# Moving work within a batch on all five engines: an attention stage with a hand-written order, Trainium2, one core

## The reference

```python
x = x + jnp.tanh(g_xattn[0]) * _L0_xattn_ref(_layernorm(x), ctx_1024, ctx_1024, w_q, b_q, w_k, b_k, w_v, b_v, w_o, b_o)
x = x + jnp.tanh(g_ffn[0]) * _L0_ffn_ref(_layernorm(x), conf_w, conf_b, gate_w, up_w, down_w, wealth)

# attention: softmax(q k^T / sqrt(16)) v per head, then w_o
# ffn:
bids = sigmoid(x @ conf_w.T + conf_b) * wealth          # (b, s, 8)
top_bids, selected = top_k(bids, 2)
combine = sum(one_hot(selected, 8) * softmax(top_bids)[..., None], axis=2)
expert_out[e] = (silu(x @ gate_w[e].T) * (x @ up_w[e].T)) @ down_w[e].T
output = einsum('ebsh,bse->bsh', expert_out, combine)
```

## Time and profile before

| | us |
|---|---|
| median of 3 runs | 1151.61 |
| lowest and highest | 1150.68, 1152.59 |
| profiled execution | 1148.98 |
| its span, first to last instruction | 1147.2 |
| prologue, to the end of the first turned maxima | 0 to 44.4 |
| batches 0 to 2 | 44.4 to 124.6 |
| one batch of the steady loop | 24.9 |
| batch 14 | 398.3 to 424 |

### The profile page before, as it was taken

The page is one execution under the profiler, slowest core; times in us unless marked ns, Lnnn a source line. Parts: engine busy times, 40 slices in busy tenths (PEclk is TensorE's granted clock), DMA queues, the critical chain, the costliest instruction groups (busy, mean ns, idle before and its releaser), DMA issues. The chain is left out here.

```text
span 1147.2 us, 24335 instructions
## 1 busy us (share of the span) xinstructions
PE 1069.5 (93%) x8310; PEld 892.5 (78%) x8310; DVE 647.4 (56%) x1575; ACT 547.4 (48%) x877; POOL 347.4 (30%) x404
## 2 busy tenths in 40 slices
PE   5789999999999978898999999999899999999994
PEld 4556767777777755575999999999579999999993
DVE  3657777777777764447444444444754444444442
ACT  4466777777777744445333333333643333333331
POOL 2024545554545552513112112112311211211211
PEclk8799999999999989999999999999999999999997
DMA  7000111111111173466212112112461211211211
GB/s 240 25 21 20 50 39 43 63 38 38 47 38 38 49 272 146 141 240 225 58 23 38 33 23 38 33 23 38 160 234 19 38 33 23 38 33 23 38 33 16
DMA packets 48426, 79.41 MB, mean 69 GB/s; under 512 B 6400, under 2 KB 42240, under 8 KB 44544
## 3 DMA queue, kind: packets, MB, share of 16 engines
q0 software_dynamic: 18080, 50.93, 16.5%
q1 hardware_dynamic: 30304, 27.95, 8.3%
HBM read 53.42 MB, written 25.18 MB: 69 GB/s over the span
## 5 line engine op out<-in xcount | busy, mean ns | idle before, releaser
L1809 POOL DMA_INDIRECT out<-y,token x64 | 103.7, 1620 | 473.3 <-DVE y L1693 352.7
L1585 ACT ACTIVATE silu<-gate 128x512 f32<-128x512 f32 x128 | 76.8, 600 | 277.0 <-PE up L1424 277.0
L960 DVE TENSOR_REDUCE max_neg<-maxps 128x4 f32<-128x1024 f32 x128 | 156.5, 1223 | 56.1 <-PE maxps L547 56.0
L1436 PE MATMUL down<-w_split,h_hi 128*128 128x512 f32 x512 | 185.8, 398 | 0.0
L1684 DVE TENSOR_TENSOR h<-silu,up 128x512 f32<-128x512 f32 x128 | 88.1, 688 | 171.0 <-ACT silu L1585 171.0
L1424 PE MATMUL gate<-x_hi,w_split 128*128 128x256 f32 x1024 | 184.1, 281 | 0.0
L1424 PE MATMUL up<-x_hi,w_split 128*128 128x256 f32 x1024 | 184.0, 281 | 0.0
L759 ACT ACTIVATE probs<-scores 128x1024 f32<-128x1024 f32 x124 | 127.3, 1026 | 86.4 <-PE scores L572 85.2
L1424 PEld LDWEIGHTS gate<-x_hi,w_split 128*128 128x128 f32 x1024 | 148.8, 188 | 2.9
L1424 PEld LDWEIGHTS up<-x_hi,w_split 128*128 128x128 f32 x1024 | 147.8, 188 | 0.0
L1438 PE MATMUL down<-w_split,h_lo 128*128 128x256 f32 x512 | 144.0, 281 | 0.0
(11 more groups left out here) (203 smaller groups left out, 1762.5 us busy)
## 6 DMA issues: line engine op xcount, KB each, us to landing
xg<-dispatched SPq DMA_DIRECT2D x39, 272.0 KB, 2.8
stage<-gate_T POOLq DMA_DIRECT2D x10, 1024.0 KB, 7.2
stage<-up_T POOLq DMA_DIRECT2D x10, 1024.0 KB, 9.4
stage<-down_T POOLq DMA_DIRECT2D x10, 1024.0 KB, 11.5
ctxT<-ctxT SPq DMA_DIRECT2D x17, 256.0 KB, 2.9
x_all<-x SPq DMA_DIRECT2D x16, 256.0 KB, 5.1
out<-x_all SPq DMA_DIRECT2D x16, 256.0 KB, 2.1
out<-y,token POOLq DMA_INDIRECT x70, 3.8
```

Of the source, the lines that this page charges most:

```text
L960: V.tensor_reduce(to, maxps[:], AX.X, ALU.max, negate=True).then_inc(s["max_taken"], 1)
L1436: mm(down[t][:].rearrange("p (n d) -> p n d", n=2), h_hi[:, i, rows], split[:, :, cols], start=i == 0, stop=False, skip_group_check=True)
L1585: nc.scalar.activation(silu[pair % 2][:], gate[pair % 2][:], ACT.Silu).then_inc(s_silu, 1)
L1809: pool.indirect_dma_start(out, bass.IndirectOffsetOnAxis(token[:, t:t + 1], axis=0), y[:, t, :], None, compute_op=ALU.add).then_inc(s_adde ...
```

## The change

The orders of the five engines' slots change; no operation is added or dropped but the places of waits.

- TensorE: `max_scores` 3 goes ahead of `score` 3, `score` 5 and `max_scores` 4 go behind the ranks, and the stack K0 behind the second group of values (`weigh` 1). `UNITS` follows: S5 now ahead of K0.
- ScalarE: the dense keys are read ahead of the third exponential instead of behind the fourth, the first values' result ahead of the fourth instead of behind the fifth, the sixth exponential ahead of K0's reading.
- VectorE: the statistics of x ahead of the first choice, and the positions ahead of the maxima of pair 5 instead of behind them.
- GpSimd: bias and contexts' split in mid-batch, ahead of the split of Q and the scatters, instead of behind both. In batch 1 the contexts' split for batch 3 goes directly behind the split of K.
- Prologue: stacks in the order K0, Q0, K1, Q1, the first maxima of batch 0 as soon as the first three are there, batch 1's norm, transpose and projections between them.

```diff
-        UNITS = ["S0", "S1", "S2", "S3", "S4", "K0", "S5", "S6", "S7", "K1", "Q0", "Q1"]
-        STACKS = ["K0", "K1", "Q0", "Q1"]
+        UNITS = ["S0", "S1", "S2", "S3", "S4", "S5", "K0", "S6", "S7", "K1", "Q0", "Q1"]
+        STACKS = ["K0", "Q0", "K1", "Q1"]
...
-            for what in STACKS:
-                stack_first(0, what)
+            stack_first(0, "K0")
+            stack_first(0, "Q0")
+            stack_first(0, "K1")
+            max_scores(0, 0, 0, 2)
+            turn_x(1, PRO1)
+            stack_first(0, "Q1")
+            max_scores(0, 0, 1, 2)
+            project_k(1, 1, PRO1)
+            max_scores(0, 0, 2, 2)
             pe.wait_ge(s["consts_loaded"], 16 * NCONST)
             pe.wait_ge(s["constants_ready"], 1)
-
             project_v(0, PRO1)
-            turn_x(1, PRO1)
-            max_scores(0, 0, 0, len(STACKS))
-            project_k(1, 1, PRO1)
-            max_scores(0, 0, 1, len(STACKS))
+            max_scores(0, 0, 3, 2)
             project_q(PRO1)
...
                 weigh(b, par, 0)
+                max_of_next(3)
                 score(b, par, 3)
-                max_of_next(3)
                 if back:
                     attn_out(use)
                 score(b, par, 4)
-                max_of_next(4)
...
                 if late:
                     ranks(b - 2, use)
+                score(b, par, 5)
+                max_of_next(4)
+                weigh(b, par, 1)
                 stack_ahead("K0")
-                weigh(b, par, 1)
                 max_of_next(5)
-                score(b, par, 5)
...
                 exps(b, 0)
                 exps(b, 1)
+                if ahead:
+                    read_k(b + 2, use)
                 exps(b, 2)
...
+                read_pv(b, 0)
                 exps(b, 3)
                 if ahead:
-                    read_k(b + 2, use)
                     norm_x(b + 2)
...
                 max_of_next(4)
-                max_of_next(5)
                 if late:
                     positions(b - 2, par, use)
+                max_of_next(5)
...
+                if isinstance(b, int) and b == 1:
+                    split_ctx(3, 1, use)
                 if back:
                     scale_of(b - 1, "scale2_chain", "ln2_stats", mv2, rstd2, shift2, "ln2_scaled")
+                if ahead:
+                    add_bias(b + 2)
+                if ahead and not is_first(b):
+                    split_ctx(b + 3, 1 - par, use)
                 if ahead:
                     split(b + 2, "Q", use, units_before(b) + (UNITS.index("Q1") + 1 - len(UNITS)))
                 if late:
                     scatter(b - 2, par)
-                if isinstance(b, int) and b == 1:
-                    split_ctx(3, 1, use)
-                if ahead and not is_first(b):
-                    split_ctx(b + 3, 1 - par, use)
-                if ahead:
-                    add_bias(b + 2)
```

More of the change, by code:

```diff
@@ L311, in attention_stage @@
         PRO0 = Use(["TX", "K", "Q"], 0)
-        PRO1 = Use(["V", "TX", "K", "Q", "MT"], after_all(PRO0))
+        PRO1 = Use(["TX", "K", "V", "Q", "MT"], after_all(PRO0))
         def without(*parts):
@@ L651, in tensor_attention @@
             project_v(0, PRO1)
-            turn_x(1, PRO1)
-            max_scores(0, 0, 0, len(STACKS))
-            project_k(1, 1, PRO1)
-            max_scores(0, 0, 1, len(STACKS))
+            max_scores(0, 0, 3, 2)
             project_q(PRO1)
-            for pair in range(2, HPAIRS):
+            pe.wait_ge(s["unit_read"], len(STACKS))
+            max_scores(0, 0, 4, len(STACKS))
+            for pair in range(5, HPAIRS):
+                stack_first(1, STACKS[pair - 5])
                 max_scores(0, 0, pair, len(STACKS))
-                if pair < 6:
-                    stack_first(1, STACKS[pair - 2])
             turn_maxima(0, PRO1)
+            stack_first(1, STACKS[3])
             def body(b, par, use, ahead, nxt, back, late):
@@ L829, in scalar_attention, with read_first_stack @@
             act.wait_ge(s["consts_made"], 1)
[L830 to L841, removed]
+            def read_first_stack(b, what):
+                read_stack(b, what[0], int(what[1]), first_stack_unit(b, what))
+            norm_x(0)
+            read_whole(xT[:], "TX", PRO0)
+            read_k(0, PRO0)
+            high_part(0, "K", PRO0)
+            read_q(0, PRO0)
+            high_part(0, "Q", PRO0)
+            read_first_stack(0, "K0")
+            norm_x(1)
+            read_first_stack(0, "Q0")
+            read_first_stack(0, "K1")
+            read_whole(xT[:], "TX", PRO1)
+            read_first_stack(0, "Q1")
+            read_k(1, PRO1)
+            high_part(1, "K", PRO1)
+            act.wait_ge(s["consts_loaded"], 16 * NCONST)
+            nc.scalar.activation(tg[:], gates[:], ACT.Tanh).then_inc(s["consts_made"], 1)
+            read_q(1, PRO1)
+            high_part(1, "Q", PRO1)
+            for what in STACKS:
+                read_first_stack(1, what)
             def body(b, par, use, ahead, nxt, back, late):
@@ L852, in body @@
                     read_whole(oT[:], "TN", use)
+                read_pv(b, 0)
                 exps(b, 3)
                 if ahead:
-                    read_k(b + 2, use)
                     norm_x(b + 2)
                 exps(b, 4)
+                exps(b, 5)
                 if late:
                     second_weight(b - 2)
-                read_pv(b, 0)
                 if ahead:
@@ L863, in body @@
                 stack_ahead("K0")
-                exps(b, 5)
                 if back:
@@ L875, in body @@
                 stack_ahead("K1")
+                stack_ahead("Q0")
                 if back:
                     sigmoid(use)
-                stack_ahead("Q0")
+                read_pv(b, 3)
                 stack_ahead("Q1")
-                read_pv(b, 3)
             def out_of_last():
@@ L1062, in vector_attention @@
             dve.wait_ge(s["constants_ready"], 1)
+            for pair in range(3):
+                maxima(0, pair)
+            rest_part(1, "K")
             dve.wait_ge(s["consts_loaded"], 16 * NCONST)
@@ L1066, in vector_attention @@
             read_v(0, PRO1)
-            for pair in range(HPAIRS):
+            maxima(0, 3)
+            maxima(0, 4)
+            rest_part(1, "Q")
+            for pair in range(5, HPAIRS):
                 maxima(0, pair)
[L1069 to L1074, removed]
+                if pair < 7:
+                    split_weights(pair - 5, "kv"[pair - 5], (wk_s, wv_s)[pair - 5])
             read_maxima(0, PRO1)
@@ L1083, in body @@
                     space_early_experts(use)
+                if ahead:
+                    stats_x(b + 2)
                 if late:
                     first_choice(b - 2)
-                if ahead:
-                    stats_x(b + 2)
                 if nxt:
```

## The result

The changed kernel is slower: 1207.29 us (median, 1206.47 to 1208.67) against 1151.14 for the kernel before; the ratio is 1.0488, 95% interval 1.0459 to 1.0517. The profiled execution took 1206.47 (span 1204.8) against 1148.98: +57.5, where the forecast had +35.8. The direction and the place were right; the time lies 7 us above the range.

A forecast was written before the change was run, and what follows sets the result against it. TensorE, busy 93% of the span, was taken as the bound. Prologue -5.0, batches 0, 1 and 14 -0.8, batch 2 -4.0 and loop +45.6 sum to +35.8: 1184.8 profiled, forecast 1187.4 us, range 1171 to 1200.

The forecast's parts named there:

- The hold: Loop batches: large GpSimd operations hold VectorE's two-SBUF-input operations in positions, delaying max_scores 6; 2.4 us a batch, order gain included.
- The small operations: GpSimd's four 128x2 operations beside positions' first operations hold nothing; charged nothing, against 0.5 us a batch by the skill.
- second_choice: VectorE, loop: the earlier K_rest holds its two-input operations, ending it about 1.0 us later; TensorE feels 0.15.
- The clock: TensorE, loop: matmuls run at 1.2 GHz behind an idle stretch of about 2.7 us; 1.4 us a batch, bounds 0 and 2.2.
- batch 2's 1.4 us: The part of batch 2's extra 3.96 us in the old trace put on the slow clock behind its 2.24 us gap.
- The order by itself: Loop batches: the new order without the GpSimd hold gains about 0.24 us a batch, bounds -0.4 and +0.1.
- K_rest's gap: TensorE's 0.35 us wait for GpSimd's K_rest ahead of the keys' first stack, forecast to go.
- the new wait of 0.3 for the fourth exponential: TensorE, loop: score 5, now close behind score 4, must wait about 0.3 us for the exponential of 4.
- Batch 2's stall: Batch 2: first_choice no longer meets the contexts' splits on GpSimd; -4.0 us, bounds -4.4 and 0.
- The prologue: Before the loop: first maxima behind three stacks bring turn_maxima from 43.44 to 38.3; -5.0 us, bounds -8 and -2.5.
- The first rival: Loop: VectorE is held but the slow clock costs nothing; 12 x 2.4 less 9.8 = +19.0, 1170.6 us; chance 0.22.
- the train: GpSimd's bias, context's high part and rest, run in sequence at 217.05 to 220.4 beside VectorE's positions in a loop batch.

The follow-up runs named there:

- e7: The changed kernel with GpSimd's contexts' split directly behind the scale of x and the bias directly behind the split of K: 1140.43 us, ratio 0.9919.
- e11: e10 with GpSimd's loop order of e7, so the old loop order on TensorE, ScalarE and VectorE: 1144.82 us, ratio 0.9939.
- e1: The changed kernel with GpSimd's bias and contexts' split put back behind the scatters in the loop batches: 1144.86 us, ratio 0.9952.
- e10: The kernel before with only the new prologue, batch 1's moved contexts' split and the statistics of x ahead of the first choice: 1142.27 us, ratio 0.9937.
- e8: The changed kernel plus four unread float32 products per loop batch in TensorE's gap ahead of max_scores 6: 1168.14 us, ratio 1.0160.
- e9: The changed kernel plus two unread float32 products per loop batch in TensorE's gap ahead of max_scores 6: 1167.82 us, ratio 1.0140.
- e5: The changed kernel with only GpSimd's bias put back behind the scatters, contexts' split left ahead of the split of Q: 1172.95 us, ratio 1.0203.
- e4: The changed kernel with only positions put back behind the maxima of pair 5: 1159.66 us, ratio 1.0068.

## Why the prediction was right in kind and wrong in size

- **The hold, right.** positions is held by the bias, the high part and the rest; also the high part, a cast, holds (0.64 to 353.04), which no row of before had shown. The forecast of 2.4 per batch, order gain included, measures 26.81 - 24.87 = 1.94. TensorE's gap is 2.2 to 2.3 (once 2.59) where 2.7 was said: three operations were caught, the others slipped through at the ends of GpSimd's, and positions took 4.6 us, not 4.9. I had named operations with two inputs in SBUF, and that was too narrow: two of the three held here, a COPY and a TENSOR_SCALAR, have one tensor as input, and so had the TENSOR_SCALAR of 0.83 us in the earlier trace rows, which I read as one with two. The size came out nearly right because operations with two inputs stand close behind them; that is argued, no run took them apart. The Trainium skill, SBUF — State Buffer, section "Who interferes with whom", has copies and tensor_scalar among those that can use the pair of ports shared with GpSimd, and TENSOR_REDUCE never; the rows agree with both: COPY 1.22 and TENSOR_SCALAR 0.64, and the reduction that runs inside the rest part of K (343.70, below) 0.17.
- **The small operations, right.** Where the first choice meets GpSimd's small operations, the comparison and its successor take 0.17 inside the 0.72 us power, as the earlier trace rows had it; beside a 128x512 operation they took 1.19 and 1.23:

```profile
335.29 0.72 POOL L1169 TENSOR_TENSOR rstd<-rstd,minus_half 128x2 f32<-128x2 f32 x1
```
```profile
335.54 0.17 DVE L999 TENSOR_TENSOR t<-bids,v 128x16 f32<-128x16 f32 x1
335.75 0.17 DVE L1001 SCALAR_TENSOR_TENSOR u<-t,eno 128x16 f32<-128x16 f32 x1
```

- **second_choice, right.** K_rest, now earlier, catches its dv (the same 0.16 as in the earlier trace rows becomes 1.08), and TensorE doesn't feel it:

```profile
343.69 1.28 POOL L1198 TENSOR_TENSOR K_rest<-K_dense,K_high 128x512 fp32r<-128x512 f32 x1 [0.15 <-POOL K_high L1196]
```
```profile
343.70 0.17 DVE L1009 TENSOR_REDUCE v<-bids 128x2 f32<-128x16 f32 x1
343.90 1.08 DVE L1010 TENSOR_TENSOR dv<-v 128x2 f32<-128x2 f32 x1
```

- **The clock, the step that failed.** "I charge batch 2's 1.4 us in each batch; bounds 0 and 2.2." It is 3.95 in a steady batch. The mechanism was right, and so was the price of a microsecond at the low clock: 1.4 for some 3.4 is 0.41, and 3.95 for some 10 is 0.39. What failed is the length, taken over from one occurrence: the slow stretch is 10 us long here, three times that of batch 2. The trace of before held a longer one, which I didn't read (windows of before):

```profile
36.00:42.00 6.00, 3.99 (x28) 3.15 (x28) 3.88 (x5) 2.05 (x2) 0.00 (x0) 0.50 0.00 0
42.00:48.00 6.00, 4.14 (x12) 2.62 (x10) 3.74 (x9) 0.00 (x0) 0.00 (x0) 0.50 0.11 36
104.00:108.00 4.00, 3.66 (x18) 3.31 (x20) 2.69 (x6) 0.00 (x0) 0.32 (x2) 0.57 0.00 0
```

The last line is the stretch that I used, (1 - 0.57) x 4 / 0.5 = 3.4 us at half clock; the first two are twelve microseconds at the lower level, in the prologue, though with TensorE waiting for a third of them. The mean clock of 0.87 over batch 14, which stands in the table of before, was a second sign: (1 - 0.87) x 25.6 / 0.5 = 6.7 us. With the longest of these, an upper bound of four times 1.4, or 5.6 a batch, would have been due, and the range would have held the result. The range was also narrower than the bounds it was made of: added up, 12 x (2.5 + 2.2) - 2.5 (prologue) + 1 (batches 0, 1 and 14) = +54.9 gives 1206.5, not 1200, and even that is 0.8 short. Why the stretch is three times as long here as in batch 2 of before isn't shown.
- **The order by itself, right in sum:** 0.22 measured for 0.24 (e7 against e11). K_rest's gap of 0.33 is gone, but the new wait of 0.3 for the fourth exponential isn't there as a gap in e7, so 0.1 goes elsewhere and the match is partly luck. **Batch 2's stall, right:** -4.0 was said; 24.86 and 25.02 instead of 28.83 in e1 and e10 make -3.8 to -4.0.
- **The prologue, right in mechanism, too large in size.** turn_maxima was to stand at 38.3; it stands at 40.60 here. In the twelve traces with this prologue it stands at 38.12 to 40.93, in the median at 39.3, so the usual gain is some 4 us and not 5.0. The earliest is e7's. The key projection of batch 1 tells the two apart (the changed kernel, then e7):

```profile
24.11 3.78 PE L479 MATMUL misc<-ctxT,wk_s 128*128 128x256 f32 x8
```
```profile
23.44 1.99 PE L479 MATMUL misc<-ctxT,wk_s 128*128 128x256 f32 x8
```

3.78 against 1.99 us: the lower clock again, in another place of the prologue from one execution to the next.

**The sum, made again** from the max_rows rows: prologue and batches 0 and 1, 92.10 - 95.72 = -3.6; batches 2 to 13, 363.2 - 302.6 = +60.6; batch 14, 24.65 - 25.60 = -0.95; the rest, 724.8 - 723.3 = +1.5: together +57.6. Of the 60.6, batch 2's stall is -4.0, hold and order 12 x 1.94 = +23.3, and +41.3 is left for the clock, where 12 x 1.4 = 16.8 was forecast: 24.5 too little. The hold was forecast 5.5 too large, and outside the loop's batches the forecast was 2.8 too low. 24.5 - 5.5 + 2.8 = 21.8 is the whole miss. 41.3 / 12 = 3.4 is under 3.95 because the first batches differ: batch 4 had its gap of 2.22 us (at 175.33) and stayed at full clock up to the next gap.

The first rival, a hold without the slow clock, was priced at 1170.6; e8 and e9, which are that case made by hand, took 1168.

## What to carry to other kernels

Before moving a large GpSimd operation, look at what VectorE does at that time: beside reductions, PSUM reads and statistics it cost nothing here, beside a chain of tiny SBUF operations it held one after another to its own end, which cost TensorE time only where an awaited maxima stood behind them. Two moves that cost 0.1 and 0.7 to 1.7 us a batch alone cost 5.9 together, so look at where they meet: here the train, positions and an awaited maxima came into one line. And take the upper bound for an idle stretch of TensorE from the longest slow stretch that the trace shows anywhere, not from the one behind the nearest gap.

## What the hardware showed that was not expected

- The slow clock cost nearly twice the idle time that came before it: 2.22 us of gap, 3.95 us of slowness, at the 1.2 GHz level for about 10 us. Two unread products in the gap (0.85 us of it) were enough to avoid nearly all of it, so the time fell by 39 us for more work.
- The size of a gap alone doesn't tell what the clock does. One of 2.22 us in batch 4 of the changed kernel was followed by no slow stretch. In e5, with two gaps of mostly 1.1 to 1.5 us in a batch, the clock fell in two of twelve batches; in e4 it fell with all four gaps of 1.31 us and behind three of eight of 0.74. What makes the difference stays open.
- Where the clock falls in some batches and not in others, times spread: nine of e4's ten lie within 17 us. Those of the changed kernel, whose steady batches all had the slow stretch, lie within 2.2, those of e9 within 0.9.
